# A Mamba-style mixer with two expert layers: TensorE's dense unit moved to the end of each tick, VectorE's taps moved behind the sums into Y

## The reference, cut to what matters

```python
zxbcdt = hidden_states @ in_proj_w.T              # gate, x, B, C, dt
xBC = silu(depthwise_conv(xBC, conv_w) + conv_b)  # 4 taps along the tokens
...
Y_diag = einsum('bhcij,bcjhd->bcihd', Gm * L, xs)               # Gm = C B^T, L = exp(segment sums)
states = einsum('bckhn,bhck,bckhd->bchdn', B, decay_states, xs)
...                                                             # states carried from chunk to chunk
Y_off  = einsum('bckhn,bchdn,bhck->bckhd', C, states, state_decay)
y = Y_diag + Y_off + D * x
y = y * silu(gate)                                              # then an RMS norm over each group
return y @ out_proj_w.T
```

## Time and profile before

| | |
|---|---|
| median of 3 runs | 2069.37 us (2069.25 to 2069.98) |
| the profiled execution, its own time | 2066.19 us |
| its span, first to last instruction | 2064.4 us |
| PE busy | 1975.3 us, 96% of the span |
| DVE, ACT, POOL busy | 1497.6, 1182.6, 1033.3 us |
| mean granted clock of PE | 0.987 of full speed |

### The profile page before, as it was taken

The page is one execution under the profiler, slowest core; times in us unless marked ns, Lnnn a source line. Parts: engine busy times, 40 slices in busy tenths (PEclk is TensorE's granted clock), DMA queues, the critical chain, the costliest instruction groups (busy, mean ns, idle before and its releaser), DMA issues.

```text
span 2064.4 us, 39384 instructions
## 1 busy us (share of the span) xinstructions
PE 1975.3 (96%) x11776; PEld 1637.7 (79%) x11776; DVE 1497.6 (73%) x2825; ACT 1182.6 (57%) x2569; POOL 1033.3 (50%) x907
## 2 busy tenths in 40 slices
PE   3899999999999999999999999999999999998998
PEld 2688878888888888888888887888788777776876
DVE  6698589859985997699669867985898571186215
ACT  3596369637953784387449645963696325432441
POOL 1288139714960595179318922881497125240433
PEclk7899999999999999999999999999999999999999
DMA  2443035203521451235134313430352049931995
GB/s 86 136 142 103 27 105 163 78 31 116 167 67 38 125 158 51 70 109 145 42 89 124 111 42 94 147 99 27 105 166 75 23 163 387 362 111 42 364 397 182
DMA packets 143909, 261.75 MB, mean 127 GB/s; under 512 B 19536, under 2 KB 35920, under 8 KB 143696
## 3 DMA queue, kind: packets, MB, share of 16 engines
q1 hardware_dynamic: 134848, 231.35, 35.3%
q0 software_dynamic: 7520, 24.65, 3.6%
q10 hardware_dynamic: 1328, 3.15, 0.4%
HBM read 233.38 MB, written 25.69 MB: 125 GB/s over the span
## 4 chain that ended last, share of the span: by engine, by line
PE 65%; issue 20%; DVE 6%; POOL 6%; ACT 1%; DMA 1%; another core or an unknown queue 0%; DVEq 0%; POOLq 0%; SPq 0%; ACTq 0%
PE bank L1602 35%; PE bank L1737 6%; PE bank L1751 5%; PE bank L1892 5%; POOL Y L728 4%; PE bank L1692 4%; PE bank L1904 3%; PE bank L1720 2%; DVE Y L1244 1%; PE bank L1879 1%; PE bank L1711 1%; PE bank L1610 1%; DVE quad L1167 1%; DVE Y L1253 1%; DVE X L1488 1%
## 5 line engine op out<-in xcount | busy, mean ns | idle before, releaser
L1602 PE MATMUL bank<-xh,wh 128*128 128x512 f32 x1288 | 524.3, 407 | 17.1 <-POOL wl L711 13.1
L1602 PE MATMUL bank<-xh,wl 128*128 128x512 f32 x1288 | 505.5, 392 | 0.0
L1602 PE MATMUL bank<-xl,wh 128*128 128x512 f32 x1288 | 502.9, 390 | 0.0
L711 POOL TENSOR_TENSOR wl<-raw,wh 128x512 fp32r<-128x512 f32 x144 | 192.3, 1340 | 486.8 <-ACT wh L886 486.8
L1244 DVE SCALAR_TENSOR_TENSOR Y<-bank,cpar,Y 128x511 f32<-128x511 f32 (+2 forms) x384 | 286.9, 747 | 22.9 <-ACT Y L932 13.8
L1602 PEld LDWEIGHTS bank<-xh,wh 128*128 128x128 f32 x1288 | 243.4, 189 | 65.2 <-issue 18.0
L1602 PEld LDWEIGHTS bank<-xh,wl 128*128 128x128 f32 x1288 | 242.5, 188 | 54.6
L1602 PEld LDWEIGHTS bank<-xl,wh 128*128 128x128 f32 x1288 | 243.8, 189 | 46.1 <-issue 0.5
L728 POOL TENSOR_TENSOR Y<-Y,gt 128x512 f32<-128x512 f32 x128 | 185.8, 1451 | 94.4 <-DVE gt L1298 92.7
L1306 DVE TENSOR_TENSOR al<-Y,ah 128x512 fp32r<-128x512 f32 x128 | 95.7, 747 | 169.1 <-ACT ah L990 169.1
L1602 PE MATMUL bank<-wh,ah 128*128 128x512 f32 x544 | 213.7, 393 | 2.4 <-DVE X L1514 1.7
(11 more groups left out here) (229 smaller groups left out, 4066.0 us busy)
## 6 DMA issues: line engine op xcount, KB each, us to landing
mem<-c_rows SPq DMA_DIRECT2D x128, 256.0 KB, 3.8
mem<-wffn_d SPq DMA_DIRECT2D x62, 512.0 KB
E<-e_rows SPq DMA_DIRECT2D x256, 96.0 KB, 3.3
raw<-wconv_d SPq DMA_DIRECT2D x80, 256.0 KB, 2.7
cv<-c_rows SPq DMA_DIRECT2D x64, 256.0 KB, 3.9
spare<-c_rows SPq DMA_DIRECT2D x64, 256.0 KB, 4.3
raw<-wgate_d SPq DMA_DIRECT2D x64, 256.0 KB, 2.7
raw<-wout_d SPq DMA_DIRECT2D x64, 256.0 KB, 2.7
```

What stands on the lines that cost most here:

```text
L711: inc(pool.tensor_tensor(wl[:, W_SLOT[p], :], raw[:, R_SLOT[p], :], wh[:, W_SLOT[p], :], ALU.subtract), w_lo)
L1602: got = mm(out, l, r, start=first and n == 0, stop=last and n == 2)
```

## The change

In PE's loop over ticks, the dense unit is moved from the head of the tick to behind C; B, the transposes of B, G, X, D and C come first. The sum of squares at tick 37 stays behind both. In DVE's loop, the column of D, ydiag and off are moved ahead of the taps and of the end of the convolution. No instruction is added or removed, and no wait's count is changed.

```diff
@@ DVE, tick k, behind S @@
+                    if k == T_X:
+                        ...                                   # dcol
+                    u = k - D_
+                    if 0 <= u < UNITS:
+                        now(dve, diag_mm, i, u + 1)
+                        ...
+                        inc(STT(dst, dst, dcol[:, pair:pair + 1], bank[DG][:, :], ALU.mult, ALU.add), ydiag_ok)
+                    u = k - C_
+                    if 0 <= u < UNITS:
+                        now(dve, off_mm, i, u + 1)
+                        e_arrived(dve, i, u)
+                        inc(STT(E[:, u % ER, :], bank[OF][:, 0:(CH - 1) * P], 0.5, E[:, u % ER, :], ALU.mult,
+                                ALU.mult), off_ok)
                     if k < NCONV:
                         ...                                   # taps of convolution k
                     kc = k - 1
                         ...                                   # end of convolution k-1
-                    if k == T_X:
-                        ...
-                    u = k - D_
-                        ...
-                    u = k - C_
-                        ...
@@ PE, tick k @@
                 for k in range(NBIG):
+                    u = k - B_
+                        ...                                   # B, transposes of B, G, X, D, C, unchanged
+                        inc(last, off_mm)
                     out = bank[big_bank(k)][:, :]
                     if k < NCONV:
                         ...                                   # dense unit of tick k
-                    u = k - B_
-                        ...
-                        inc(last, off_mm)
                     if k == NORM_AT - 1:
```

More of the change, by code:

```diff
@@ L1235, in _ @@
                             inc(last, s_step if c < CH - 2 else s_ok)
[L1237 to L1253, removed]
                     if k == T_X:
@@ L1276, in _ @@
                                 ALU.mult), off_ok)
+                    if k < NCONV:
+                        tile, b = conv_unit(k)
+                        dst = piece(tile, b)
+                        now(dve, tap0, i, k + 1)
+                        for s in range(1, TAPS):
+                            if s > 1:
+                                now(dve, taps, i, 3 * k + s - 1)
+                            last = STT(dst[:, s:SEQ], bank[big_bank(k)][:, 0:SEQ - s],
+                                       cpar[:, tile, TAPS - 1 - s:TAPS - s], dst[:, s:SEQ], ALU.mult, ALU.add)
+                            inc(last, taps)
+                    kc = k - 1
+                    if 0 <= kc < NCONV:
+                        tile, b = conv_unit(kc)
+                        dst = piece(tile, b)
+                        now(dve, conv_th, i, kc + 1)
+                        inc(STT(dst, bank[big_bank(kc)][:, :], 1.0, dst, ALU.add, ALU.mult), conv_ok)
                     u = k - A_ - 1
@@ L1644, in _ @@
                 for k in range(NBIG):
[L1645 to L1679, removed]
                     u = k - B_
@@ L1753, in _ @@
                         inc(last, off_mm)
+                    out = bank[big_bank(k)][:, :]
+                    if k < NCONV:
+                        tile, b = conv_unit(k)
+                        s = W_SLOT[tile]
+                        if b == 0:
+                            piece_split(pe, i, tile)
+                        big_bank_free(pe, i, k)
+                        for kt in range(KT):
+                            last = three(out, xh[:, kt, b * SEQ:(b + 1) * SEQ], xl[:, kt, b * SEQ:(b + 1) * SEQ],
+                                         wh[:, s, kt * P:(kt + 1) * P], wl[:, s, kt * P:(kt + 1) * P],
+                                         kt == 0, kt == KT - 1, False)
+                        inc(last, big_mm)
+                    elif k < NCONV + NGATE:
+                        tile, b = gate_unit(k)
+                        half, col = tile // 4, tile % 4 * P
+                        if tile % 4 == 0 and b == 0:
+                            piece_split(pe, i, CONV + KT * half + KT - 1)
+                        big_bank_free(pe, i, k)
+                        for kt in range(KT):
+                            s = W_SLOT[CONV + KT * half + kt]
+                            last = three(out, xh[:, kt, b * SEQ:(b + 1) * SEQ], xl[:, kt, b * SEQ:(b + 1) * SEQ],
+                                         wh[:, s, col:col + P], wl[:, s, col:col + P], kt == 0, kt == KT - 1, False)
+                        inc(last, big_mm)
+                    else:
+                        t = k - NCONV - NGATE
+                        big_bank_free(pe, i, k)
+                        for m in range(2):
+                            now(pe, y_lo, i, 2 * t + m + 1)
+                            for j in range(4):
+                                if t == 0:
+                                    piece_split(pe, i, PIECES - XT + 4 * m + j)
+                                s = W_SLOT[PIECES - XT + 4 * m + j]
+                                last = three(out, ah[:, m, j, :], al[:, m, j, :], wh[:, s, :], wl[:, s, :],
+                                             m == 0 and j == 0, m == 1 and j == 3, True)
+                            inc(last, big_mm if m else out_half)
                     if k == NORM_AT - 1:
```

## The result

The changed kernel took 2152.05 us (median of 4 runs, 2151.25 to 2154.52), the kernel before 2069.68 us beside it: 1.040 times as long, 95% interval 1.0382 to 1.0418. That is 82.4 us more; 95.6 were forecast. The profiled execution took 2151.3 us. In what follows e(k) is again the end of PE's dense unit of tick k.

What follows compares the result with a forecast made beforehand. PE was taken to bound the kernel, busy 1975.3 of 2064.4 us. Entry 2.8, chain 5.35, tick 21 1.0 and clock 2.8 make 11.95 us a group, 95.6 for 8; 2069.4 + 95.6 = 2165 us, range 2115 to 2190.

Steps and rivals of the forecast that it cites:

- the only wait that comes back: Mixer before the change: one PE wait comes back, at B(0)'s start, once in each of 8 groups, 9.9 us in all.
- Entry: Tick 10: B(0) waits for the end of convolution 8; idle 4.05 us instead of 1.24, loss 2.8 us per group.
- The chain of two ticks: Ticks 11 to 20: D waits for POOL's products through xs, 1.07 us every second tick, 5.35 us per group.
- B behind S: Ticks 11 to 20: B needs S of the tick before, ready just when PE arrives; no more than 0.1 us.
- D of tick 21: D waits for the product DVE makes in tick 20 behind the end of convolution 19: loss 1.0 us per group.
- The clock: After the entry's idle time PE runs at half for 5.4 to 5.9 us from B(0): 2.8 us lost per group.
- the clock did not hold: Rival: the clock holds through PE's 4.05 us of idle time at the entry; 2142 us, chance 0.20.
- The chain did not vanish: Rival: only the entry costs, xs or the products go earlier and the chain vanishes; 2092 to 2114 us, chance 0.11.
- The gaps of 0.17 us before D and C: Rival: PE's weight-load gaps before D and C are DVE's late sums, removing 41 us; 2050 us, chance 0.03.
- Tick 16: POOL has two weight parts, 1.29 us each, swallowed by its idle time; nothing added, bound 1.3 us a group.

Runs made afterwards that it cites:

- e9: The change with end of convolution (DVE) and its tanh (ACT) ahead of taps and first tap from tick 9 on only: 2107.65 us, ratio 1.0228.
- e10: The change with end and tanh first from tick 9 on, xs one tick earlier, weight parts at ticks 14, 15, 16: 2097.12 us, ratio 1.0166.
- e11: PE's old order, DVE's new one, with end of convolution and tanh first from tick 9 on: 2050.4 us, ratio 0.9942 to the kernel before.
- e12: The kernel before with only end of convolution and tanh first from tick 9 on: 2057.14 us, ratio 0.9966.
- e4: The change with xs of a unit made one tick earlier on DVE, between the sums into Y and the taps: 2129.76 us, ratio 1.0313.
- e3: The change with 12 more matmuls, result unused, ahead of B(0) in tick 10 to keep PE working: 2136.36 us, ratio 1.0342.
- e2: DVE's new order with PE's old one: 2060.41 us against 2064.9 for the kernel before, ratio 0.9983.
- e5: The change with end of convolution k-1 ahead of the taps of k on DVE, its tanh ahead of the first tap on ACT: 2148.9 us, ratio 1.0393.
- e8: PE's old order, DVE's new one, with end of convolution and tanh first in all ticks: 2101.21 us, ratio 1.0154 to the kernel before.
- e1: PE's new order with DVE's old one (sums into Y behind taps and end of convolution): 2496.07 us, one run.

## Why the prediction was right, and where its sizes were off

- **Direction and mechanism**: right. Forecast 2165 us, measured 2152.05, inside the range; the loss is 82.4 us, 0.86 of the forecast. The three stalls named in it are the three in the list of waits, with the engines and lines that it gave. The sizes that were off by 0.1 us or more were all too high, so the sum doesn't owe its fit to errors that cancel. One reading was wrong without an effect: B(0)'s is not the only wait that comes back in the mixer before. PE also waits for a weight's low part (L711) at the first dense unit of the seven later groups, 0.64 to 0.92 us, and after the change 0.66 to 0.98 us.
- **Entry**: forecast 4.05 us of idle time, measured 4.06. Loss 2.82 us a group. e9 and e10 show that it hangs on what stands ahead of the end of convolution 8 and of xs(0) on DVE: with the end ahead of the taps it falls to 2.4 us. In e11 and e12, where PE has a dense unit to do meanwhile, it is gone.
- **The chain of two ticks**: forecast 1.07 us a pair with D at e(k) + 7.86; measured 12.53 - 11.52 = 1.01, D at e(10) + 7.80, in every second tick as told. Five pairs, 5.0 us instead of 5.35. e4 takes xs out of it, and it goes. Of the 1.01 us the list of waits gives 0.74 to D itself. B of tick 12 also starts 0.13 us later behind its dense unit than B of tick 13 does (319.38 and 326.02), a little over the 0.1 that the prediction allowed for B behind S.
- **D of tick 21**: forecast 1.0 us, measured 0.61 (6.37 from D to D instead of 5.76), since the product of DVE took 1.10 us here, in each of the 8 groups, and not 1.55; why it is shorter no run shows:

```profile
376.76 1.10 DVE L1285 TENSOR_TENSOR cv<-cv,quad 128x512 f32<-128x512 f32 x1
```

- **The clock**: this term was mis-sized. Forecast 2.8 us a group, measured 1.9 (B(0) to e(10): 5.72 to 6.56, mean 6.00, less 4.11). That it falls in each group was right, and e3 confirms the cost by taking it away. What failed was "PE at half for the first 5.4 to 5.9 us after B(0) starts": in five groups it was half for only 3.4 us, from 0.5 to 1.2 us behind B(0)'s start on, as the window 308.60 to 312.00 shows, and in the other three it was half from B(0)'s start for 4.7 to 5.2 us. The Trainium skill, "TensorE: Matmul & The Clock Gate", section "HAM oscillation — how this bites in real kernels", says that waits between bursts of matmuls put the array back to half rate, so that each burst starts cold. The trace agrees that the clock falls in all 8 groups, but only in 3 of them did PE's work start at the half level; in the other 5 the fall came 0.5 to 1.2 us behind.
- **Sum**: 2.82 + 5.03 + 0.61 + 1.89 = 10.35 us a group, of 10.43 between two B(0).
- **Rivals**: the clock did not hold. The chain did not vanish. The gaps of 0.17 us before D and C are not late sums: in e2 the sums come ahead of the taps, the gaps stay, and PE's ticks still take 5.76 us. Tick 16 was named and costed at nothing; in the change it was indeed hidden by the chain's other stalls, and came out only when these were gone.

## What to carry to other kernels

In a software pipeline whose engines are both full, moving one engine's work within a tick changes how many ticks lie between maker and user of each value. Walk each wait from its maker through every in-order engine on its way, and count the chain's length in ticks of the bound engine: a chain that spans two ticks and is 1 us too long shows as a stall in every second tick. Look at the first and last tick of each stage on their own, since there the order that suits the steady ticks can be wrong (e5, e8). And test the halves of a change one by one: here DVE's half alone was a small gain, PE's half alone cost 431 us, and with DVE's half beside it 82.

## What the runs showed of the hardware

PE's clock fell after, or late in, 4.06 us of idle time in 8 of 8 groups. With 2.42 to 2.51 us it fell in 4 of 8 groups (e9) and with 2.43 or 2.44 us in 8 of 8 (e10). With 1.24 and 1.34 us it never fell (before, e3). Between, the length of the idle time alone does not decide: in e9 the two groups with 2.51 us kept the clock, and of the six with 2.42 or 2.43 us four lost it. When the idle time was longer, the fall could come early in it: in the seventh group of the kernel after, PE's last matmul ended at 1344.33, the clock stood at 1.00 up to 1346.2 and at 0.50 from 1346.3 on, 2.1 us before B(0). I had not expected it for a wait as short as 2.4 us, and it made the smaller stalls of e9 and e10 dearer than their length. In e1 idle times of 3.5 us in a row let it fall again and again: PE's busy time grew by 159 us for the same matmuls.
